# Reordering the first stage of an RWKV and mixture-of-experts kernel at its ends: rounds 0, 1 and last, with a gate product moved amid the next batch's mixes

## The reference

```python
xn = layernorm(x)                                # B, T, C = 8, 512, 512
prev = concat([xn[:, 1:2], xn[:, :-1]], axis=1)
xx = prev - xn
r = sigmoid((xn + xx * tm_r) @ Wr.T)
k = (xn + xx * tm_k) @ Wk.T
v = (xn + xx * tm_v) @ Wv.T
g = sigmoid((xn + xx * tm_g) @ Wg.T)
attn = r * wkv_scan(exp(k), v) * g @ Wo.T        # then a layernorm with ln_g, ln_b
z = rmsnorm(xn) * w_norm
probs = softmax(z @ w_router)                    # 32 experts, top 4 of each token, at most 256 tokens each
out = x + attn + experts(z) + shared_expert(z) + xn
```

## Time and profile before

| what | us |
|---|---|
| three runs | 1670.83, 1667.74, 1669.04; median 1669.04 |
| the profiled execution, whole | 1669.34 |
| its span, first to last instruction | 1667.5 |
| PE busy in the span | 1632.4 |
| DVE busy | 1313.3 |
| POOL busy | 820.5 |
| ACT busy | 729.5 |
| first stage (until the first expert's products) | about the first 429 |

### The profile page before, as it was taken

One profiled execution on the slowest core, in us unless ns is written; L12 is line 12 of the kernel. 1 busy time (PEld: TensorE's weight loads), 2 busy tenths in 40 slices (PEclk: granted clock), 3 DMA queues, 4 the chain that ended last, 5 costly groups with the idle time before them and its releaser, 6 DMA issues.

```text
span 1667.5 us, 26386 instructions
## 1 busy us (share of the span) xinstructions
PE 1632.4 (98%) x8384; PEld 1388.7 (83%) x8384; DVE 1313.3 (79%) x1927; ACT 729.5 (44%) x1312; POOL 820.5 (49%) x722
## 2 busy tenths in 40 slices
PE   6999999999999999999999999999999999999999
PEld 5777888887999999999987888888888888888887
DVE  7988999988777777766789687776868768687776
ACT  5746555653777777777743121121211212112121
POOL 4488777775445454544445353352424425243351
PEclk9999999999999999999999999999999999999999
DMA  4544334334787777777686555554644343433431
GB/s 165 200 148 173 132 146 156 118 135 181 263 275 277 277 275 267 263 263 247 246 280 224 172 190 154 202 162 165 190 148 145 116 151 116 145 118 116 160 103 47
DMA packets 119781, 304.83 MB, mean 183 GB/s; under 512 B 20172, under 2 KB 25804, under 8 KB 115088
## 3 DMA queue, kind: packets, MB, share of 16 engines
q1 hardware_dynamic: 100464, 269.59, 45.7%
q0 software_dynamic: 18944, 33.66, 7.0%
q10 hardware_dynamic: 288, 0.52, 0.1%
HBM read 239.11 MB, written 81.35 MB: 192 GB/s over the span
## 4 chain that ended last, share of the span: by engine, by line
PE 75%; DVE 15%; issue 6%; ACT 2%; POOL 2%; DMA 0%; DVEq 0%; POOLq 0%; ACTq 0%; SPq 0%
PE bank L2240 26%; PE bank L1459 14%; PE bank L2254 13%; PE bank L1502 8%; PE bank L2271 5%; PE bank L1028 5%; DVE mixf L723 3%; PE bank L1452 2%; PE bank L1468 2%; DVE bank L691 1%; DVE st L671 1%; DVE mix L730 1%; DVE zT_lo L698 1%; DVE s_wg L2091 1%; PE bank L962 1%
## 5 line engine op out<-in xcount | busy, mean ns | idle before, releaser
L1028 PE MATMUL bank<-mix,w 128*128 128x512 f32 x1488 | 353.0, 394 | 9.6 <-DVE ekv L739 4.9
L1028 PEld LDWEIGHTS bank<-mix,w 128*128 128x128 f32 x1488 | 277.1, 189 | 72.2 <-DVE ekv L739 5.5
L2240 PE MATMUL bank<-s_zT,s_wu 128*128 128x512 f32 x1056 | 254.3, 390 | 4.1 <-DVE bank L1996 4.0
L2254 PE MATMUL bank<-s_wd,s_h 128*128 128x512 f32 x1056 | 253.7, 389 | 0.7 <-DVE s_h L2002 0.7
L2240 PE MATMUL bank<-s_zT,s_wg 128*128 128x512 f32 x1056 | 253.6, 389 | 0.0
L2240 PEld LDWEIGHTS bank<-s_zT,s_wu 128*128 128x128 f32 x1056 | 197.7, 188 | 47.4 <-issue 6.4
L2254 PEld LDWEIGHTS bank<-s_wd,s_h 128*128 128x128 f32 x1056 | 198.1, 188 | 42.3 <-DVE s_h L2002 1.2
L2240 PEld LDWEIGHTS bank<-s_zT,s_wg 128*128 128x128 f32 x1056 | 198.2, 188 | 41.2
L1244 POOL TENSOR_TENSOR e_wg<-e_g_in,e_wg 128x768 fp32r<-128x768 f32 x62 | 114.0, 1860 | 152.1 <-ACT e_wg L1271 151.4
L1785 POOL DMA_INDIRECT s_picked<-y_rows,s_slot x128 | 140.1, 1094 | 83.6 <-DVE s_total L2052 44.8
L1889 ACT ACTIVATE s_act_g<-bank 128x512 f32<-128x512 f32 x88 | 52.6, 598 | 289.9 <-PE bank L2240 289.9
(11 more groups left out here) (196 smaller groups left out, 2613.8 us busy)
## 6 DMA issues: line engine op xcount, KB each, us to landing
s_wu<-wu_split SPq DMA_DIRECT2D x88, 512.0 KB, 3.5
e_g_in<-in_w_first SPq DMA_DIRECT2D x32, 768.0 KB, 5.0
e_u_in<-in_w_second SPq DMA_DIRECT2D x32, 640.0 KB, 6.4
e_d_in<-in_w_down SPq DMA_DIRECT2D x32, 512.0 KB, 6.9
y_rows<-e_y SPq DMA_DIRECT2D x32, 512.0 KB, 2.9
s_zT<-zT_parts SPq DMA_DIRECT2D x16, 1024.0 KB, 6.7
zT_parts<-zT_hi SPq DMA_DIRECT2D x8, 1024.0 KB, 6.3
zT_parts<-zT_lo SPq DMA_DIRECT2D x8, 1024.0 KB, 8.5
```

The costliest lines, as they stand in the source:

```text
L1028: last = pe.matmul(pj[m][:], w[i][:, w_part, k, m * P:(m + 1) * P], mix[:, i % 2, k, x_part, :], start=(k == 0 and q == 0), stop=(k == KC ...
L2240: last = pe.matmul(into[:], w[:, w_part, k, :], zT[:, x_part, k, :], start=(q == 0 and k == 0), stop=(q == 2 and k == KC - 1))
L2254: last = pe.matmul(yp[j][:], h[:, i, h_part, j * P:(j + 1) * P], wd[f][:, w_part, :], start=(f == 0 and q == 0), stop=(f == NFS - 1 and q ...
```

## The change

Seven edits, all in the order of instructions; one wait is added, and no arithmetic changes.

1. Round 0, POOL: `weight_lo(G_)` waits until the lo parts of R are made (by DVE).
2. Round 0, DVE: ekv 2 and 3 go ahead of the four mixes of G.
3. Round 0, DVE and ACT: `gates(0, 0)` goes amid the mixes of K of batch 1 (after two of four) and out of `make_zT`; ACT's `gate_g(0, 0)` and `(0, 1)` go ahead of its `mix_hi` of K of batch 1.
4. Round 1, DVE: the product of `assign(0)`, now `place_among(0)`, goes ahead of the lo parts of V.
5. Round 1: the lo parts of R go from POOL to DVE, two ahead of ekv 0, 1 and `choose`, two after ekv 2, 3; POOL issues 12 scatters of batch 0 in a row instead.
6. Last round, DVE, PE and ACT: ekv 2 and 3 go into `fill_parts`, ahead of `place`; `fill` goes behind the whole of R on PE; two mixes of G, one lo part and the reading of the table go ahead of `fill_table`; `first_gate_up` goes ahead of ACT's `mix_hi` of G.
7. Last round, PE: `first_turn` goes from k = 1 to k = 2 of G's second half.

```diff
@@ gpsimd, first_round @@
             norm_scales(1, 1)
+            pool.wait_ge(lo_made, (R_ + 1) * KC)
             weight_lo(G_)
@@ gpsimd, one_round @@
             if second:
                 norm_scales(b + 1, 1 - half)
-                scatter(b - 1, 1 - half, 0, MORE)
-                mix_lo_among(b, R_, b - 1, 1 - half, MORE, last)
-                scatter(b - 1, 1 - half, MORE + KC, last - KC)
+                scatter(b - 1, 1 - half, 0, last - KC)
@@ scalar, first_round @@
             route_exp(0)
-            for k in range(KC):
-                mix_hi(1, K_, k)
             gate_g(0, 0)
             gate_g(0, 1)
+            for k in range(KC):
+                mix_hi(1, K_, k)
@@ scalar, last_round @@
             gate_r(LAST, 1)
+            first_gate_up()
             for k in range(KC):
                 mix_hi(LAST, G_, k)
             gate_r(LAST, 2)
             gate_r(LAST, 3)
-            first_gate_up()
             first_down()
@@ vector: the product of assign becomes place_among(b) @@
-        def fill_parts():
+        def fill_parts(between):
...
             fill.step(dve.tensor_tensor(near_far[:, :, 0], valid[:], near_far[:, :, 1], ALU.subtract))
+            between()
             dve.tensor_tensor(place[:], ...
+        def read_table():
+            dve.wait_ge(table_loaded, 16)
+            fill.step(dve.tensor_copy(table_f[:], keep["table"][:]))
         def fill_table():
-            dve.wait_ge(table_loaded, 16)
-            fill.link(dve.tensor_copy(table_f[:], keep["table"][:]))
+            fill.join()
             dve.wait_ge(filled, 1)
@@ vector, first_round @@
-            for k in range(KC):
-                make_mix(0, 0, G_, k)
             make_ekv(0, 2)
             make_ekv(0, 3)
+            for k in range(KC):
+                make_mix(0, 0, G_, k)
...
             for k in range(KC):
+                if k == 2:
+                    gates(0, 0)
                 make_mix(1, 1, K_, k)
-            make_zT(1, 1, lambda: gates(0, 0))
+            make_zT(1, 1)
@@ vector, one_round @@
+            if second:
+                place_among(0)
             for k in range(KC):
                 mix_lo(b, V_, k)
             if second:
-                assign(0, 0, 0)
+                assign(0, 0, 0, placed_among=True)
...
-            choose(b)
-            for m in range(KC):
-                make_ekv(b, m)
+            if second:
+                mix_lo(b, R_, 0)
+                mix_lo(b, R_, 1)
+                make_ekv(b, 0)
+                make_ekv(b, 1)
+                choose(b)
+                make_ekv(b, 2)
+                make_ekv(b, 3)
+                mix_lo(b, R_, 2)
+                mix_lo(b, R_, 3)
+            else:
+                choose(b)
+                for m in range(KC):
+                    make_ekv(b, m)
@@ vector, last_round @@
-            fill_parts()
-            make_ekv(LAST, 2)
-            make_ekv(LAST, 3)
+            fill_parts(lambda: (make_ekv(LAST, 2), make_ekv(LAST, 3)))
+            make_mix(LAST, FIRST_HALF, G_, 0)
+            read_table()
+            make_mix(LAST, FIRST_HALF, G_, 1)
+            mix_lo(LAST, G_, 0)
             fill_table()
             first_index()
-            for k in range(KC):
+            for k in range(2, KC):
                 make_mix(LAST, FIRST_HALF, G_, k)
-                if k:
-                    mix_lo(LAST, G_, k - 1)
+                mix_lo(LAST, G_, k - 1)
             mix_lo(LAST, G_, KC - 1)
@@ tensor, last_round @@
-            project(LAST, R_, 1, {1: fill})
+            project(LAST, R_, 1)
+            fill()
             project(LAST, G_, 0)
-            project(LAST, G_, 1, {1: first_turn})
+            project(LAST, G_, 1, {2: first_turn})
```

More of the change, by code:

```diff
@@ L579, in first_round @@
             route_exp(0)
+            gate_g(0, 0)
+            gate_g(0, 1)
             for k in range(KC):
                 mix_hi(1, K_, k)
-            gate_g(0, 0)
-            gate_g(0, 1)
             for k in range(KC):
@@ L776, in choose, with place_among @@
             dve.tensor_scalar(token_id, token_id, float(T), None, ALU.add)
-        def assign(b, half, uses, product=oh):
-            route.round(b, CHOOSE)
+        def place_among(b, product=oh):
             dve.wait_ge(chosen_made, b + 1)
@@ L786, in assign @@
                               ALU.mult).then_inc(pos_read, 1)
+        def assign(b, half, uses, product=oh, placed_among=False):
+            route.round(b, CHOOSE)
+            if not placed_among:
+                place_among(b, product)
             dve.wait_ge(pos_read, b + 1)
@@ L876, in first_round @@
             mix_lo(0, R_, KC - 1)
+            make_ekv(0, 2)
+            make_ekv(0, 3)
             for k in range(KC):
                 make_mix(0, 0, G_, k)
-            make_ekv(0, 2)
-            make_ekv(0, 3)
             dve.tensor_copy(before[:], before_in).then_inc(setup_dve, 1)
```

## The result

| what | before, us | after, us |
|---|---|---|
| median of six runs each, by turns | 1669.51 (1667.74 to 1670.83) | 1659.87 (1659.39 to 1663.82) |
| the profiled execution | 1669.34 | 1659.39 |
| its span | 1667.5 | 1657.6 |

The ratio of after to before is 0.9948, with a 95% interval of 0.9938 to 0.9958: faster by 9.6 us, where 9.2 were forecast. All ratios here are of fast executions alone: one of 1829.96 us of e10 and one of 8512.1 us of the kernel before, beside it, are not in them.

A forecast was written before the change was run, and what follows sets the result against it. PE was taken to bound every stage, so only its idle time could be won. Rounds 0 and 1 (5.6) plus the last round (3.6) gave 9.2 us off 1669.34, so 1660.1 us, range 1657.8 to 1664.2.

The forecast's parts named there:

- the 17 us that set batch 2: Round 1, DVE: time from `assign`'s product to the gate product, taken as 17 between 15.5 and 18.0; batch 2 at 121.9.
- Round 0: First round: PE gets back its waits for R's lo part and ekv, overlaps and slow matmuls, 2.9 us.
- Without that cover, the DVE chain passes one for one: Round 0, rest of `make_zT` before `score`: the gate order costs nothing with 0.2 to spare; otherwise lateness passes in full.
- not as said: Rival, round 0: POOL's added wait is already met when reached; gain some 1 us less, 1661 us; chance 0.01.
- a stall of 1.8 before the `turn_xn`: Round 1, PE's third `turn_xn`: wanted at 95.0, comes at 96.8 behind ACT's `route_exp` and `keep_turned`; new stall 1.8 us.
- The table load: Round 0, ACT before `gate_g`: load without the skill's 1.38 us drain; with drains, up to 1.7 us comes off.
- Round 1: Second round: early product nets 0.9, four lo-part waits go (3.7); with round 0, batch 2 starts 5.6 us earlier.
- the 0.6 of stall: Round 1, G: POOL's fourth lo part ends at 114.0, PE wants it at 113.4; stall of 0.6 us.
- The loop: Rounds 2 to 6, unedited: all engines move by the same 5.6 us, so the cost is zero.
- The slower rival's phase shift: Rival, loop rounds: POOL against DVE in another phase brings waits at G's `mix_lo`, 18.5 us in all; 1679 us, chance 0.05.
- The last round: Last round: 5.1 won, less new stalls of 0.95, 0.4 and 0.1, gives 3.6 us, between 2.4 and 4.1.
- The 5.1 for the stall and its clock: Last round: moving ekv 2 and 3 ahead removes the 3.23 us stall, 0.15 overlap and 1.7 of half clock.

The follow-up runs named there:

- e10: Changed kernel, round 1 with `keep_turned` before `route_exp`, gate products amid K's mixes, two scatters after POOL's K lo parts; last round G's third mix before `fill_table`: 1664.25 us.
- e5: Changed kernel with edit 3 undone (first two gate products of batch 0 back in `make_zT`, `gate_g` behind ACT's mixes of K): 1661.33 us in one run.
- e3: Changed kernel without POOL's added wait in round 0 (edit 1 undone): 1661.44 us in one run.
- e8: Changed kernel with ekv 2 and 3 of the last round back behind `column`, the rest of edits 6 and 7 kept: 1674.25 us in one run.
- e12: The changed kernel itself, unedited, run again on another chip: 1665.25 us, ratio to before 0.9948.
- e6: Changed kernel with ACT's first two `keep_turned` ahead of `route_exp` in round 1: 1662.7 us in one run.
- e9: Changed kernel with the first two gate products amid K's mixes and `gate_g` ahead of ACT's in round 1 too: 1666.31 us in one run.

## Why the prediction was right

- **The sizes.** The two edited stretches gained 5.75 + 4.02 = 9.8 us where 9.2 were forecast, by the waits that the prediction names. That each came so near is in part luck: the 17 us that set batch 2 were a choice between 15.5 and 18.0, several terms below missed in opposite ways, and one fall of the clock in the unedited output stage shifts an execution by more than the distance between 9.2 and 9.6.
- **Round 0** stands, but its parts were priced as if each passed through. All waits went, and `score` came 66.66 - 63.84 = 2.8 us earlier (2.9 forecast). What a part is worth at batch 2 is another matter: the added wait 0.2 of its 0.9, the gate order about 1.7 of its 3.8, in e5's one execution. The prediction gave the gate order only as a thing to be covered, at no cost; undone, it costs a wait of 1.97 and a half clock. "Without that cover, the DVE chain passes one for one" was wrong: more than one for one at first, by the clock, and then half absorbed.
- **The rival "not as said"** said 1 us less without the wait; it is 0.2. The step that failed is that it counted DVE's blocking in full, though the same text expected a stall of 1.8 before the `turn_xn`, in which such a gain is lost.
- **The table load.** After, ACT loads the table for `route_exp` and again for `gate_g`:

```profile
59.47 1.28 ACT L525 ACT_TABLE_LOAD   x1
60.76 0.33 ACT L525 ACTIVATE ex<-sh 128x148 f32<-128x148 f32 x1
61.11 1.28 ACT L520 ACT_TABLE_LOAD   x1
...
63.12 1.26 ACT L520 ACTIVATE bank<-bank 128x512 f32<-128x512 f32 x2 [0.73 <-PE bank L1053]
```

  The activation starts 0.01 us after the load ends, as the forecast took it, and `gate_g` then waits 0.73 for PE. The Trainium skill (ScalarE: Activation LUTs, What ACT_TABLE_LOAD costs) adds a drain of 1.38 us; no such gap stands between these rows.
- **Round 1.** `place_among` ahead of V's lo parts did what was said. `sh` ended at 95.30 (95.8 forecast, of which the earlier start explains 0.5), the new stall is 1.41 (1.8). The twelve scatters took 16.3 (16.9), G's fourth lo part ended at 112.76 (114.0), and the 0.6 of stall did not come. It was a slip of the sum as well: with the stall of 1.8 in it, PE wants that part at 119.70 - 3.75 - 3.7 + 1.8 = 114.05 and not at 113.4, and ends G at 121.0 and not at 120.7. From `assign`'s product to the gate product it took 120.51 - 103.86 = 16.65 (17, between ends of 15.5 and 18.0). Batch 2 came at 121.25, 5.75 earlier apart from the start-up, against 5.6. The wait of 1.04 on DVE's gate product says that DVE sets it (the forecast implies 121.9 - 120.7 = 1.2, or 0.9 with the sum put right), and in e3, where the product of `assign` starts 0.16 later, batch 2 is 0.20 later.
- **The loop** kept it: 0.16 lost of 5.75. The slower rival's phase shift did not come; PE's window shows 259.77 busy of 262 us.
- **The last round** gave 4.02 against 3.6. The 5.1 for the stall and its clock is what its reversal cost (3.52 and 1.6). The 0.8 for the second lo part is 0.73. Of the small terms two did not come: `first_turn` (0.4) and the turned rows (0.1). The gathered rows had landed at 414.69, and PE asked at 414.88; that cover is 0.2 us.
- **Left open:** why signals came late on two of the chips, what the stall of 1.41 costs where they don't, what edit 3 is worth when the clock doesn't fall, and whether the third mix of G is worth 0.1 or 0.5.

## What to carry to other kernels

Price an edit at the landmark behind the next place where another engine is pinned, not where its own stall stands: here 0.9 and 3.8 us won by PE were worth 0.2 and 1.7 there, and edits 1 to 3 brought 1.24 alone but 5.75 with 4 and 5, which move the next pin. Behind a long wait of PE add the clock to the price, here 1.6 to 1.7 us, but as a chance: it came behind four of five waits of 2.38 us and more, behind 10 of 17 of 1.90 to 1.99, and behind none of 30 of 1.1 to 1.8. Read a single run by stretches: its total can be led by stretches that the edit doesn't touch, here by a fall of the clock that one execution has and the next has not.

## What the runs showed of the hardware

- **Whether the clock falls behind a wait of some 1.9 us differs from one execution to the next.** Past the start-up, in the fourteen traces, the granted clock fell to 0.50 (1.2 GHz) behind idle stretches of PE of 3.23, 3.25, 2.82 and 3.52 us, and not behind 2.38 in e8, where 24 matmuls took 5.72. It stayed at 1.00 behind the 1.41 of after, the 1.67 of before and all others of 1.1 to 1.8. Between 1.90 and 1.99 it fell in 10 cases and stayed in 7. Fourteen of these are one and the same wait of the output stage, which every kernel here has between 904 and 916 us, and behind which it fell in seven of the fourteen. This is PE at that wait in after and in e12, which are the same kernel, and then e12's window:

```profile
904.68 2.99 PE L2266 MATMUL bank<-s_zT,s_wu 128*128 128x512 f32 x12 [1.92 <-DVE bank L2022]
```

```profile
909.10 4.24 PE L2266 MATMUL bank<-s_zT,s_wu 128*128 128x512 f32 x12 [1.93 <-DVE bank L2022]
```

```profile
910.60:913.90 3.30, 3.30 (x9) 2.65 (x8) 3.30 (x2) 1.02 (x2) 1.37 (x1) 0.50 0.29 108
```

  With the next twelve, 3.31 instead of 2.88, the fall cost 1.7 us. So neither the length alone nor the kernel decides. The prediction had only the 3.23 and the 1.67. The window behind e5's 1.97, part of it at either level:

```profile
72.00:75.00 3.00, 3.00 (x10) 2.36 (x9) 2.93 (x5) 0.89 (x3) 0.00 (x0) 0.62 0.00 0
```

- **Signals came late on two chips.** The change showed no such gap on its first chip and gaps of 3.1, 4.8 and 6.9 us in e12, each time where ACT or DVE waited for PE while PE went on; e5 and e6 had them near `count` of round 1 (3.5 and 2.3) and none in the last round, which took them 33.60 and 33.65 on the chip where e9 took 37.27. In e12 they cost 37.29 - 33.54 = 3.75 us in the last round and 0.7 at batch 2. Its ratio to before was still 0.9948, as before stood at 1674.07 there; whether that kernel had late signals too, no trace shows. What causes them no run here tells.
- **Small DVE instructions wait for POOL's tensor work, not for its indirect DMAs.** With lo parts of POOL beside them, operations on 16 elements or fewer took 1.86, 2.00 and 1.87 us; during the twelve scatters DVE's kept their usual times (`sh` 0.17). Each of the three ended within 0.05 us of the end of a lo part of POOL; each also began 0.5 to 0.7 us before that part's record does, while a scatter stood in POOL's, so the line between the two is not sharp. The Trainium skill (SBUF — State Buffer, Who interferes with whom) has VectorE and GpSimd share one port pair as an exclusive lock, held for the whole instruction; with POOL's lo parts at 1.3 us each the trace agrees.
